# Reordering the first batch's adapter and the copies of its first weights

## The chip, the cores and the metric

The kernel runs on one NeuronCore of a Trainium2 chip. The metric is the device time of one execution in microseconds, as the median of a few executions. Five engines work side by side, each with its own instruction stream: TensorE (PE; PEld is its weight load), VectorE (DVE), ScalarE (ACT), GpSimd (POOL) and SyncE (SP). They order themselves with semaphores. DMAs are issued here by SyncE and ScalarE.

## What is computed

The input `x` is (4, 512, 256) in float32. Four stages, each with a residual, are applied one after the other; weights are picked by small index inputs, one index to a batch element:

```python
# L0: adapter of a language, then a layer norm
h = relu(x @ W1[lang] + b1[lang])                 # (512, 64)
a = x + h @ W2[lang] + b2[lang]                   # (512, 256)
x = x + layernorm(a) * gamma[lang] + beta[lang]
# L1: a linear layer of a subject
x = x + (x @ weight[subj].T + bias[subj])
# L2: two experts and three shared nets (256 -> 1024 -> 256, relu between), gated
x = x + sum_of_nets(x)
# L3: attention pooling with a prefix, postfix or cloze mask
x = x + masked_pooling(x)
```

Only the first batch element's L0 and L1, and the loading of its first L2 weights, are touched by the change.

## The kernel before

**Stages.** The four batch elements run one after the other. A batch is `SLOTS` = 40 slots of L2 work (5 nets times 8 chunks of 128 hidden units). In each slot TensorE computes one chunk of the hidden layer (`first_product`, into `ps_hid`) and, two slots later, what that chunk adds to the output (`second_product`, into `ps_net`). The L0 and L1 stages of the next batch and L3 of the one before are woven into the slots. All large products are made of three matmuls on split operands: each operand is a `hi` part (rounded to float32r) and a `lo` part (the rest), and hi·hi, lo·hi and hi·lo are summed. So every chunk of hidden values is split by ScalarE (`hid_hi`, with the relu) and VectorE (`hid_lo`), and every pair of weight chunks by ScalarE (`wi_hi`, `wo_hi`) and GpSimd (`wi_lo`, `wo_lo`).

**Weights.** SyncE loads them by halves of a net (four chunks, 512 KB of wi into `raw_wi` and 512 KB of wo into `raw_wo`), into two slots in turn (`load_half`, L458 to L471). A pair of chunks is split by `split_weights` on ScalarE (L1074) and GpSimd. The very first half is issued by ScalarE (L1175, L1176) in the prologue, and its two pairs are copied by `first_wi` and `first_wo`. SyncE waits for both transfers of that half (`raw_in[0]`, L484) before it issues the second half at L470; before that it has loaded the first batch's parameters (`load_params`, L422 to L430, which begins with two register loads of an index), the subject's index and bias (`load_subject`, L433 to L438, again two register loads) and the small resident arrays (`load_resident`).

**The prologue.** L0 and L1 of the first batch cannot be woven into anything, so each engine has a `prologue`. It works on two halves `h` of 256 rows, that is four row tiles `r` of 128 (half 0 has tiles 0 and 1, half 1 has 2 and 3):

- TensorE transposes x (`transpose_half`, L558), computes the adapter's first product of a half (`adapter_hidden`, L638, 64 output columns, float32 in four passes) and the second product of a tile (`adapted_rows`). Even tiles get x added by TensorE with an identity matmul (L646); odd tiles get it from VectorE. Before the change it does half 0's first product, tiles 0 and 1, then half 1's first product, tiles 2 and 3. Then it transposes the subject's weights (L565, L567), transposes the normalised rows of half 0, runs three warm-up matmuls on zeros (`keep_warm`, L687), and computes the subject product `x2_part` (L666) and the first chunks of L2 for each half.
- ScalarE copies the transposed x to SBUF (`x1T`, L1147), applies bias and relu (`adapter_hidden`, L1151, writes `hT`), adds beta to the transposed x (`x_beta`, L1155, writes `xbT`), normalises the even tiles (`normalise`, L1161), copies the transposed subject weights (L1183), splits the first weights (L1164, L1169) and evacuates the subject product as `x2T_hi` (L1194).
- VectorE computes the statistics of a tile (`statistics`, L1740 adds x for odd tiles, L1743), the variance of a half (`variance`, L1749 to L1753), normalises the odd tiles (L1758), adds the normalised values to `xbT` (`add_norm`, L1763, writes `x1T`) and writes `x2T_lo` (L1771).
- GpSimd computes `rstd` and `neg_shift` of a half (L1945, L1947), then `wi_lo` and `wo_lo` of the first weights.

**What sets the order.** It is written out by hand. Each engine's instructions run in program order; each step increments a semaphore, and `Steps` turns a step's name into the count to wait for, so the strings of names (`p_pe`, `p_act`, `p_dve`) must list the steps in the order in which each engine does them.

**The small parameters.** In the first slots of batch 0 VectorE computes gate probabilities and mask parameters (`parameters(slot)`, L1651 to L1705) on tiny tiles of 128x4. Each of these steps waits for the one before. The memset of `mix_done` (L1679) tells ScalarE that the experts' scales are ready, for which ScalarE waits before it writes `wo_hi` of an expert (L1085). VectorE does `hid_lo` of a slot (L1823) in between, in program order. GpSimd, after the third pair of weights, sets up constants (L1957 to L1971), and then goes on with the pairs.

## Time and profile before

| | us |
|---|---|
| median of 3 runs | 502.25 (502.12 to 503.63) |
| the profiled execution, its own time | 501.93 |
| its span, from the first to the last instruction | 500.1 |
| PE busy, share of the span | 493.7, 99% |
| DVE busy | 349.2, 70% |
| ACT busy | 260.9, 52% |
| POOL busy | 235.8, 47% |

The span is the stretch between the first and the last instruction; 1.83 us of the execution's time lie around it. Busy times overlap, since the engines run side by side. Matmuls are pipelined, so the busy time of a group of matmuls ends after the next group has begun; the spacing of starts tells the pace. Rows of a timeline give the start, the length, the engine, the line, the operation, output<-input with shapes, how many instructions were merged (x4), and in brackets how long the engine was idle before and who ended that. What ended a wait is inferred from semaphores.

### The profile page before, as it was taken

To read this page: it belongs to the slowest core of one execution; us is meant where nothing else is said; L and a number is where in the kernel's file an instruction comes from. 1 tells how busy PE (TensorE), PEld (TensorE's weight loads), DVE (VectorE), ACT (ScalarE), POOL (GpSimd) and SP (SyncE) were. 2 spreads that over 40 slices of the span, in tenths; PEclk is the share of its full clock that TensorE was granted. 3 is DMA by queue.
4 is the path that set the end of the run, shared out by engine and by line. 5 is a ranking of instruction groups with operands and counts; after the bars stand their busy time and mean duration, and the time that the engine had idled before them with its cause. 6 is when DMAs were issued, how large, how long until landed. Compare 5 with 4: busy or idle time off the path is not lost.

```text
span 500.1 us, 7007 instructions
## 1 busy us (share of the span) xinstructions
PE 493.7 (99%) x2327; PEld 408.6 (82%) x2327; DVE 349.2 (70%) x703; ACT 260.9 (52%) x507; POOL 235.8 (47%) x201
## 2 busy tenths in 40 slices
PE   8999999999999999999999999999999999999996
PEld 5788888888888888888888888888888888888984
DVE  5687226884687799785578689788468779644477
ACT  4655554443457574535346666444345757445234
POOL 1684455445354446444644437444535444745022
PEclk9999999999999999999999999999999999999999
DMA  5865454222265442422227453422222342330002
GB/s 156 185 184 148 111 154 142 86 85 85 86 128 141 116 112 86 127 83 89 80 90 185 105 178 107 127 84 85 85 85 85 102 109 84 102 132 22 0 1 84
DMA packets 77657, 52.97 MB, mean 106 GB/s; under 512 B 40758, under 2 KB 67382, under 8 KB 77622
## 3 DMA queue, kind: packets, MB, share of 16 engines
q1 hardware_dynamic: 75734, 50.44, 35.6%
q10 hardware_dynamic: 1888, 2.10, 1.4%
q8 instruction: 18, 0.29, 0.2%
q14 instruction: 17, 0.14, 0.1%
HBM read 48.33 MB, written 2.10 MB: 101 GB/s over the span
## 4 chain that ended last, share of the span: by engine, by line
PE 98%; DVE 1%; ACT 1%; issue 0%; POOL 0%; DVEq 0%
PE ps_hid L838 14%; PE ps_hid L839 14%; PE ps_hid L843 14%; PE ps_net L900 14%; PE ps_net L895 14%; PE ps_net L896 14%; PE ps_net L867 2%; PE ps_side L537 1%; PE ps_side L541 1%; PE ps_side L536 1%; PE ps_side L547 1%; PE ps_side L550 1%; PE ps_hid L687 1%; PE ps_side L730 1%; PE ps_net L666 1%; PE ps_hid L638 0%
## 5 line engine op out<-in xcount | busy, mean ns | idle before, releaser
L1915 POOL TENSOR_TENSOR wi_lo<-raw_wi,wi_hi 128x512 fp32r<-128x512 f32 x77 | 101.6, 1319 | 207.0 <-ACT wo_hi L1088 109.8
L1109 ACT ACTIVATE hid_hi<-ps_hid 128x512 fp32r<-128x512 f32 x160 | 95.5, 598 | 194.9 <-PE ps_hid L843 193.1
L1823 DVE SCALAR_TENSOR_TENSOR hid_lo<-ps_hid,hid_hi 128x512 fp32r<-128x512 f32 x160 | 109.8, 688 | 114.0 <-ACT hid_hi L1109 112.8
L838 PE MATMUL ps_hid<-x2T_hi,wi_lo 128*128 128x512 f32 (+1 forms) x332 | 125.8, 381 | 0.0
L839 PE MATMUL ps_hid<-x2T_hi,wi_hi 128*128 128x512 f32 (+1 forms) x332 | 125.3, 379 | 0.0
L895 PE MATMUL ps_net<-hid_hi,wo_hi 128*128 128x512 f32 x304 | 118.9, 391 | 0.0
L896 PE MATMUL ps_net<-hid_hi,wo_lo 128*128 128x512 f32 x304 | 118.4, 390 | 0.0
L1916 POOL TENSOR_TENSOR wo_lo<-raw_wo,wo_hi 128x512 fp32r<-128x512 f32 x77 | 104.1, 1352 | 0.0
L843 PE MATMUL ps_hid<-x2T_lo,wi_hi 128*128 128x512 f32 (+1 forms) x332 | 98.9, 379 | 0.0
L900 PE MATMUL ps_net<-hid_lo,wo_hi 128*128 128x512 f32 x304 | 94.0, 390 | 0.0
L839 PEld LDWEIGHTS ps_hid<-x2T_hi,wi_hi 128*128 128x128 f32 x332 | 62.5, 188 | 11.8
L838 PEld LDWEIGHTS ps_hid<-x2T_hi,wi_lo 128*128 128x128 f32 x332 | 62.5, 188 | 11.7
L843 PEld LDWEIGHTS ps_hid<-x2T_lo,wi_hi 128*128 128x128 f32 x332 | 61.3, 188 | 11.8
L900 PEld LDWEIGHTS ps_net<-hid_lo,wo_hi 128*128 128x128 f32 x304 | 57.0, 188 | 12.4 <-DVE hid_lo L1823 0.4
L895 PEld LDWEIGHTS ps_net<-hid_hi,wo_hi 128*128 128x128 f32 x304 | 57.1, 188 | 11.6
L896 PEld LDWEIGHTS ps_net<-hid_hi,wo_lo 128*128 128x128 f32 x304 | 57.1, 188 | 11.5
L1081 ACT ACTIVATE wi_hi<-raw_wi 128x512 fp32r<-128x512 f32 x78 | 48.8, 626 | 1.5 <-DMA raw_wo<-in_L_cond_expert_wo_dram 1.1
L1088 ACT ACTIVATE wo_hi<-raw_wo 128x512 fp32r<-128x512 f32 x46 | 28.6, 622 | 0.0
L1085 ACT ACTIVATE wo_hi<-raw_wo,par 128x512 fp32r<-128x512 f32 x32 | 23.0, 719 | 1.7 <-DVE mix_done L1679 1.7
L1086 ACT ACTIVATE raw_wo<-raw_wo,par 128x512 f32<-128x512 f32 x32 | 22.9, 716 | 0.0
L1383 DVE SCALAR_TENSOR_TENSOR x3T<-netT,gates,x3T 128x512 f32<-128x512 f32 x24 | 19.5, 854 | 0.1
L1811 DVE SCALAR_TENSOR_TENSOR gate_acc<-gate_w,netT,gate_acc 128x256 f32<-128x256 f32 x26 | 17.5, 673 | 1.8
(330 smaller groups left out, 502.7 us busy)
## 6 DMA issues: line engine op xcount, KB each, us to landing
raw_wi<-in_L_cond_share_wi_dram SPq DMA_DIRECT2D x23, 512.0 KB, 3.8
raw_wo<-in_L_cond_share_wo_dram SPq DMA_DIRECT2D x23, 512.0 KB, 4.8
raw_wi<-in_L_cond_expert_wi_dram SPq DMA_DIRECT2D x16, 512.0 KB, 3.8
raw_wo<-in_L_cond_expert_wo_dram SPq DMA_DIRECT2D x16, 512.0 KB, 4.8
next_x2T<-in_x_dram SPq DMA_DIRECT2D x24, 64.0 KB, 4.3
x_rows<-in_x_dram SPq DMA_DIRECT2D x3, 512.0 KB, 4.0
x_rows<-netT SPq DMA_DIRECT2D x48, 32.0 KB, 2.0
out_dram<-out_rows SPq DMA_DIRECT2D x5, 256.0 KB, 5.6
```

The lines of the kernel that those rows point to most:

```text
L838: mm(dst, wi_lo[:, w, k, c], x2T_hi[:, k, rows], start=(k == 0), stop=False)
L839: mm(dst, wi_hi[:, w, k, c], x2T_hi[:, k, rows], start=False, stop=False)
L843: last = mm(dst, wi_hi[:, w, k, c], x2T_lo[:, k, rows], start=False, stop=(k == KD - 1))
L895: mm(dst, wo_hi[:, w, q % 2, cols], hid_hi[:, slot], start=opens, stop=False)
L896: mm(dst, wo_lo[:, w, q % 2, cols], hid_hi[:, slot], start=False, stop=False)
L900: last = mm(dst, wo_hi[:, w, q % 2, cols], hid_lo[:, slot], start=False, stop=closes)
L1081: fn(wi_hi[:, w], raw_wi[:, half % 2, :, c], ACT.Copy)
L1088: fn(wo_hi[:, w], raw, ACT.Copy).then_inc(w_hi_ready, 1)
L1109: fn(hid_hi[:, ring(b, q)], ps_hid[:, ring(b, q)], ACT.Relu).then_inc(hid_hi_ready, 1)
L1823: v.scalar_tensor_tensor(out=hid_lo[:, ring(b, q)], in0=ps_hid[:, ring(b, q)], scalar=0.0, in1=f32(hid_hi[:, ring(b, q)]), op0=ALU.max, op ...
L1915: g.tensor_tensor(wi_lo[:, w], raw_wi[:, half % 2, :, c], f32(wi_hi[:, w]), ALU.subtract)
L1916: g.tensor_tensor(wo_lo[:, w], raw_wo[:, half % 2, t], f32(wo_hi[:, w]), ALU.subtract).then_inc(w_lo_ready, 1)
```

## The change

On TensorE the first product of half 1 follows directly on that of half 0; then come the second products in the order tile 1, 0, 3, 2. The wait for hT of a half moves from the even tile to the odd one, which is now first. VectorE takes the statistics in the order 1, 0, variance of half 0, 3, 2, normalise of half 0, variance of half 1. ScalarE does both halves' relu first and `x_beta` of both after, issues the loads of the subject's weights and of the first wi before it waits for the first product, and issues the load of the first wo after the relu of half 0. The first wi and wo get a semaphore each (`first_raw_wi`, `first_raw_wo`), so that the counts of `raw_in[0]` start with the third half. The first copy of wi moves ahead of the normalising of half 1. The three warm-up matmuls become two.

```diff
-    WARM_XT, WARM_SUBJ = 6, 3
+    WARM_XT, WARM_NORM = 6, 2
...
+        first_raw_wi, first_raw_wo = sem("first_raw_wi"), sem("first_raw_wo")
...
-        p_pe = Steps(sem("p_pe"), "xT0 xT1 hid0 adapt0 adapt1 hid1 adapt2 adapt3 subj_wT normT0 normT1 y0 y1")
-        p_act = Steps(sem("p_act"), "xT0 xT1 hid0 xb0 hid1 xb1 norm0 subj_wT norm1")
-        p_dve = Steps(sem("p_dve"), "stats0 sum1 stats1 aggr0 var_eps0 stats2 norm0 sum3 stats3 aggr1 var_eps1 x1T00 x1T01 norm1 x1T10 x1T11")
+        p_pe = Steps(sem("p_pe"), "xT0 xT1 hid0 hid1 adapt1 adapt0 adapt3 adapt2 subj_wT normT0 normT1 y0 y1")
+        p_act = Steps(sem("p_act"), "xT0 xT1 hid0 hid1 xb0 xb1 norm0 subj_wT norm1")
+        p_dve = Steps(sem("p_dve"), "sum1 stats1 stats0 aggr0 var_eps0 sum3 stats3 stats2 norm0 aggr1 var_eps1 x1T00 x1T01 norm1 x1T10 x1T11")
...
                         load_resident()
-                        sp.wait_ge(raw_in[0], 32)
+                        sp.wait_ge(first_raw_wi, 16)
+                        sp.wait_ge(first_raw_wo, 16)
...
                 for h in range(2):
                     adapter_hidden(h)
-                    for r in (2 * h, 2 * h + 1):
+                for h in range(2):
+                    for r in (2 * h + 1, 2 * h):
                         adapted_rows(r)
...
                 normalised_rows(0)
-                keep_warm(WARM_SUBJ, warm)
+                keep_warm(WARM_NORM, warm)
...
                 if r % 2 == 0:
-                    if r == 2:
-                        pe.wait_ge(p_act.sem, p_act.at(0, "hid0"))
                     mm(adapted_bank(r), ident[:], x_rows[:, r], start=True, stop=False)
+                else:
                     pe.wait_ge(p_act.sem, p_act.at(0, f"hid{r // 2}"))
-                    if r == 0:
-                        pe.wait_ge(zeros_ready, 3)
-                        pe.wait_ge(w2_in, 16)
-                        pe.wait_ge(b2_in, 16)
+                if r == 1:
+                    pe.wait_ge(zeros_ready, 3)
+                    pe.wait_ge(w2_in, 16)
+                    pe.wait_ge(b2_in, 16)
...
-                act.wait_ge(raw_in[half % 2], 32 * ((HALVES // 2) * b + half // 2 + 1))
+                if not (isinstance(b, int) and b == 0 and half == 0):
+                    act.wait_ge(raw_in[half % 2], 32 * ((HALVES // 2) * b + half // 2 + half % 2))
...
+            act.dma_start(subj_w[:], ...).then_inc(subj_in, 16)
+            net, cols = NET_AT[0] - 2, slice(0, F // 2)
+            act.dma_start(raw_wi[:, 0], ...).then_inc(first_raw_wi, 16)
             act.wait_ge(b1_in, 16)
             adapter_hidden(0)
-            act.dma_start(subj_w[:], ...).then_inc(subj_in, 16)
-            net, cols = NET_AT[0] - 2, slice(0, F // 2)
-            act.dma_start(raw_wi[:, 0], ...).then_inc(raw_in[0], 16)
-            act.dma_start(raw_wo[:, 0], ...).then_inc(raw_in[0], 16)
+            act.dma_start(raw_wo[:, 0], ...).then_inc(first_raw_wo, 16)
+            adapter_hidden(1)
             act.wait_ge(beta_in, 16)
             x_beta(0)
-            adapter_hidden(1)
             x_beta(1)
             normalise(0)
             act.wait_ge(p_pe.sem, p_pe.at(0, "subj_wT"))
             fn(first_subj_wT.rearrange("p k d -> p (k d)"), ps_net[:, 2], ACT.Copy).then_inc(p_act.sem, 1)
+            act.wait_ge(first_raw_wi, 16)
+            first_wi(0)
             normalise(1)
-            act.wait_ge(raw_in[0], 32)
-            first_wi(0)
+            act.wait_ge(first_raw_wo, 16)
             first_wo(0)
             first_wi(1)
             first_wo(1)
...
                 def variance(h):
...
-                    here(f"stats{2 * h + 1}")
+                    here(f"stats{2 * h}")
...
+                statistics(1)
                 statistics(0)
-                statistics(1)
                 variance(0)
+                statistics(3)
                 statistics(2)
                 normalise(0)
-                statistics(3)
                 variance(1)
```

## Rows read from the trace of the kernel before

**Rows 1.** The page's first part: busy us, share of the span, instructions.

```profile
PE 493.7 (99%) x2327; PEld 408.6 (82%) x2327; DVE 349.2 (70%) x703; ACT 260.9 (52%) x507; POOL 235.8 (47%) x201
```

**Rows 2.** Timeline, 5 to 20 us: start, us, engine, line, operation, [idle before <- releaser].

```profile
5.60 1.08 PE L638 MATMUL ps_hid<-x1T,w 128*64 128x256 f32 x4 [0.18 <-ACT x1T L1147]
7.30 1.13 PE L652 MATMUL ps_net<-w2b,hT 65*128 65x256 f32 x4
8.11 0.43 DVE L1743 BATCH_NORM_STATS2 stats<-ps_net 128x6 f32<-128x256 f32 x1 [3.12 <-PE ps_net L652]
8.36 1.08 PE L638 MATMUL ps_hid<-x1T,w 128*64 128x256 f32 x4
9.75 0.16 DVE L1753 TENSOR_SCALAR var_eps<-aggr 128x2 f32<-128x2 f32 x1
11.07 0.56 ACT L1161 ACTIVATE norm<-ps_net,neg_shift,rstd 128x256 f32<-128x256 f32 x1 [0.41 <-POOL neg_shift L1947]
12.74 0.87 DVE L1763 SCALAR_TENSOR_TENSOR x1T<-ps_side,gamma,xbT 128x256 f32<-128x256 f32 x2
13.36 1.10 PE L666 MATMUL ps_net<-x1T,out_rows 128*128 128x256 f32 x4 [0.26 <-DVE x1T L1763]
13.64 0.41 DVE L1758 TENSOR_SCALAR norm<-norm,aggr,rstd 128x256 f32<-128x256 f32 x1
13.91 0.56 ACT L1161 ACTIVATE norm<-ps_hid,neg_shift,rstd 128x256 f32<-128x256 f32 x1 [1.26 <-POOL neg_shift L1947]
14.62 0.63 PE L558 MATMUL ps_side<-ident,norm 128*128 128x128 f32 x4 [0.16 <-ACT norm L1161]
16.46 0.82 ACT L1194 ACTIVATE x2T_hi<-ps_net,subj_b 128x256 fp32r<-128x256 f32 x2
17.88 0.84 ACT L1194 ACTIVATE x2T_hi<-ps_net,subj_b 128x256 fp32r<-128x256 f32 x2 [0.60 <-PE ps_net L666]
```

**Rows 3.** Timeline, 21 to 39 us, of ScalarE, POOL and VectorE.

```profile
21.96 0.63 ACT L1081 ACTIVATE wi_hi<-raw_wi 128x512 fp32r<-128x512 f32 x1 [0.35 <-DMA raw_wo<-in_L_cond_share_wo_dram]
...
29.95 1.29 POOL L1916 TENSOR_TENSOR wo_lo<-raw_wo,wo_hi 128x512 fp32r<-128x512 f32 x1
...
31.89 0.72 ACT L1085 ACTIVATE wo_hi<-raw_wo,par 128x512 fp32r<-128x512 f32 x1 [1.65 <-DVE mix_done L1679]
...
37.26 1.28 POOL L1916 TENSOR_TENSOR wo_lo<-raw_wo,wo_hi 128x512 fp32r<-128x512 f32 x1
...
37.36 1.21 DVE L1692 SCALAR_TENSOR_TENSOR par<-onehot,jcol,par 128x4 f32<-128x4 f32 x1
...
38.80 0.69 DVE L1823 SCALAR_TENSOR_TENSOR hid_lo<-ps_hid,hid_hi 128x512 fp32r<-128x512 f32 x1
```

**Rows 4.** The chain that ended last, 36 to 40 us: start, us, what.

```profile
36.87 0.45 PE ps_net L900 x2
...
39.59 0.69 PE ps_net L900 x2
```

**Rows 5.** Waits of SyncE's queue, 0 to 24 us: total us, times, longest us.

```profile
SPq L470 <- DMA raw_wo<-in_L_cond_share_wo_dram: 0.4, 1, 0.4
```

**Rows 6.** Timeline of the DMA issues of the first two halves of wi.

```profile
7.35 0.50 ACTq L1175 DMA_DIRECT2D raw_wi<-in_L_cond_share_wi_dram  x1
...
13.84 0.37 SPq L470 DMA_DIRECT2D raw_wi<-in_L_cond_share_wi_dram  x1
```

**Rows 7.** The page's DMA issues: KB each, median us from issue to landing.

```profile
raw_wi<-in_L_cond_share_wi_dram ACTq DMA_DIRECT2D x1, 512.0 KB, 5.0
```

**Rows 8.** Line L433, all batches: ns min/median/max, first and last start.

```profile
L433 SPq TENSOR_LOAD <-in_itok_B_dram_ptr x4: 1244/2490/2636, 6.6 to 296.4; - x4
L433 SPq TENSOR_LOAD <-in_itok_B_dram x4: 458/462/818, 7.9 to 299.2; - x4
```

**Rows 9.** Timeline of the two bursts of warm-up matmuls.

```profile
1.32 2.74 PE L687 MATMUL ps_hid<-edge_diag 128*128 128x512 bf16 x6 [1.32 <-DVE edge_diag L1847]
...
12.29 0.81 PE L687 MATMUL ps_hid<-edge_diag 128*128 128x512 bf16 x3
```

More of the change, by code:

```diff
@@ L1169, in first_wo @@
                 fn(wo_hi[:, p], raw_wo[:, 0, 2 * p:2 * (p + 1)], ACT.Copy).then_inc(w_hi_ready, 1)
+            act.dma_start(subj_w[:], L1_weight[bass.ds(subj, 1)].rearrange("o (k p) d -> p (o k) d", p=P)).then_inc(subj_in, 16)
+            net, cols = NET_AT[0] - 2, slice(0, F // 2)
+            act.dma_start(raw_wi[:, 0], L2_share_wi[net:net + 1, :, cols].rearrange("o (k p) f -> p (o k) f", p=P)).then_inc(first_raw_wi, 16)
             act.wait_ge(b1_in, 16)
             adapter_hidden(0)
-            act.dma_start(subj_w[:], L1_weight[bass.ds(subj, 1)].rearrange("o (k p) d -> p (o k) d", p=P)).then_inc(subj_in, 16)
-            net, cols = NET_AT[0] - 2, slice(0, F // 2)
-            act.dma_start(raw_wi[:, 0], L2_share_wi[net:net + 1, :, cols].rearrange("o (k p) f -> p (o k) f", p=P)).then_inc(raw_in[0], 16)
-            act.dma_start(raw_wo[:, 0], L2_share_wo[net:net + 1, cols].rearrange("o (c p) d -> p (o c) d", p=P)).then_inc(raw_in[0], 16)
+            act.dma_start(raw_wo[:, 0], L2_share_wo[net:net + 1, cols].rearrange("o (c p) d -> p (o c) d", p=P)).then_inc(first_raw_wo, 16)
+            adapter_hidden(1)
             act.wait_ge(beta_in, 16)
             x_beta(0)
-            adapter_hidden(1)
             x_beta(1)
```

## The prediction

> **What bounds the kernel now.** I read four views, in this order. The page's first part says which engine is full: TensorE is busy for 493.7 us of a span of 500.1 [rows 1], so a gain can only come from what TensorE idles or waits, and the change touches only the first 20 us. The timeline of those 20 us comes next: the reader is to see which start stands right behind a wait. TensorE begins the adapter's first product of half 0 at 5.60 and that of half 1 at 8.36. The normalising of half 1 is late: ScalarE sat idle for 1.26 us before it at 13.91, and TensorE's transposes of half 1 start behind it at 14.62 [rows 2]. So half 1 is the late one, by what its statistics cost after 8.36. Then the chain of waits further on: TensorE's product with hid_lo at 39.59 takes 0.69 us where the one before it took 0.45 [rows 4], a stall of 0.24 us outside the changed code. And last the queue that loads weights, SyncE's: it waited 0.4 us for the first half of wo before it could issue the second half of the weights at 13.84 [rows 5, 6].
>
> **The sum for the prologue, half 0.** The first product of half 1 (four passes) now stands between hid0 and the adapter rows. The wait for hT of half 0, which ended at 7.30, was partly idle for TensorE; the four passes of half 1, 0.22 us apart and with the array already set to 64 columns, come at 6.5 to 7.2, and the adapter can begin at 7.47. The first adapter tile (now the odd one) took from 7.30 to 8.11 to reach VectorE and now reaches it at about 8.28 [rows 2]. The same VectorE operations stand between that and var_eps of half 0: 8.11 to 9.91 is 1.80 us, so it ends at 10.08, 0.17 later, and ScalarE's normalising goes from 11.07 to 11.24. The identity pass of tile 0 hid the wait for hT before; it now lies behind tile 1 and is covered by VectorE's 0.8 us of work on tile 1. ScalarE ends at 11.80, and with the 0.15 us between that and TensorE's start (13.91 plus 0.56 to 14.62) the transposes run from 11.96 to about 12.60. Before, VectorE could take x1T of half 0 only at 12.74, held by its own statistics of half 1; now those are done and it starts at 12.70. TensorE's first subject product moves from 13.36 to 13.32: a gain of 0.04 us.
>
> **Half 1.** VectorE goes on with tiles 3 and 2 without a wait, because their products are ready by 9.5 and 10.4. By the 1.80 us of half 0, begun at 9.99 and with one normalising of about 0.3 (its pace in the pipeline) in between, var_eps of half 1 is done at 12.0 to 12.1. From there to ScalarE's start POOL takes 1.16 us or less (9.91 to 11.07), so ScalarE starts at 13.1 to 13.2 instead of 13.91 and is done at 13.7 [rows 2]. VectorE's share of it is queued behind x1T of half 0: 12.70 plus 0.80 plus 0.41 is 13.91 [rows 2]. Both are ready before TensorE has issued the four passes it began at 13.32, so the transposes of half 1 follow at 14.26 instead of 14.62, and what is behind them moves by 0.39 with the refill of the array that the wait cost. **The prologue's sum is 0.39 us.**
>
> **The weight copies.** ScalarE reaches the first copy of wi at about 12.2. Issued with subj_w right after the second x1T copy, wi leaves at about 6.0 instead of 7.35, and lands 5.0 us later, at 11.0 [rows 6, 7]. The copies end at 15.1 instead of 16.46, so the first evacuation of x2T no longer waits for ScalarE: 15.84 [rows 2]. TensorE's short wait behind that in the first halves goes, but then the last part of half 1 decides: its evacuation began at 17.88, as soon as TensorE was done, and it keeps its length. It moves by 0.39 and no more, so I cost the copies' move at nothing beyond the 0.39. If ScalarE were still behind, it would hold 0.6 us. Three semaphore waits are split or moved, one warm-up pass is dropped (0.22 us, in a gap), and no instruction of the steady part changes: nothing.
>
> **Where the 0.39 us goes.** This is what decides, so I followed the stall at 39.59 back. It is TensorE waiting for VectorE's hid_lo of 38.80. VectorE came to that only after the parameter operation of 37.36, which takes 1.21 us on 128x4 elements and ends within 0.03 us of POOL's operation of 37.26 (1.28 us) [rows 3]. POOL's work comes behind ScalarE's weight copies, those behind wo_hi at 31.89, which waited for VectorE's mix_done, and that behind parameter steps that stood beside POOL's operation of 29.95; POOL's series and VectorE's both begin with ScalarE's copy of 21.96, which waited for a DMA: the second half of wo [rows 3]. From that landing to 39.5 there is no step that waits for TensorE. So TensorE meets hid_lo at 39.5 however early it arrives: it comes 0.39 earlier and stalls 0.24 plus 0.39. The weight pairs before it (POOL's series for slot 6 ends at 31.24) hang on the same landing. **What moves the end is when the second half of wo lands.** The most that could be gained is 0.63 us.
>
> **The landing.** SyncE issues that load at 13.84 because it waited 0.4 us [rows 5, 6]; the first wo is now issued about 1 us sooner and should be in by 13, so this wait goes: 0.37 earlier. Against it: SyncE's two loads of the subject index (L433), from 6.59 to 8.68 before, now run beside the transfers of subj_w and wi. In this run the pair took 1.24 and 0.82 us in the prologue, and 2.64 and 0.46 at the most in later batches, where weights were in flight [rows 8]. Bounds: 0 (or a gain of 0.3, were each load as short as its shortest row allows) and 1.04 us later, the sum of both longest against now. I take 0.3, nearer the prologue's rows since only ScalarE's queue is full there. The sum is 0.37 minus 0.3, so 0.07 us earlier, with ends at 0.63 earlier and 0.67 later.
>
> The trace shows the operations of 37.26 and 37.36 ending together [rows 3]. The Trainium skill, SBUF — State Buffer, Who interferes with whom, says that VectorE and GpSimd share a pair of ports as an exclusive lock, and that the one that comes second blocks fully. By that rule, with which the trace agrees, the order of the two starts decides: a step of VectorE that came first would take its own 0.2 us instead of 1.2, and hid_lo would come up to 1 us sooner, which is one way into rival A. A rule that speaks against the change is in DMA: Bandwidth & Descriptors, Issuing engines are not separate DMA queues: transfers issued from different engines run on the same DMA engines and interleave. By it, wi sent sooner from ScalarE slows what SyncE has under way; no row here shows the two together, and the sum would be rival B's.
>
> **The numbers.** The profiled execution took 501.93 us, its span 500.1, so 1.83 lie around it; it stands 0.32 under the median of 502.25. 501.93 minus 0.07 is 501.86, and on the scale of the median 502.2 us.
>
> **Rivals.** A: the chain from the landing is earlier after all (SyncE not slowed, or a step of VectorE of about 0.2 us, as the small one of 9.75 [rows 2] takes, starts ahead of POOL's operation and not behind it), and the gain survives. For it: SyncE's wait of 0.4 is real [rows 5]. Against: everything in the chain is in program order. Gain 0.3 to 0.63: 501.6 to 501.9. B, on the other side: the second half of the weights lands later. Its place is L433 and its price up to 1.04 us against the 0.37; it decides from where SyncE arrives at L470 after 13.84, that is once the two index loads take over 0.4 us more than now. It then shows in full, as a longer stall at hid_lo: up to 0.67, 502.9. C: TensorE's clock falls in the prologue. The burst of six at 1.32 takes 0.46 us each, the three at 12.29 take 0.27 [rows 9]: the lower and the upper of the two levels (1.2 and 2.4 GHz). The lower one was over by the four passes of 5.60, which take the 1.08 us of those of 8.36 [rows 2], so it held for at most 4.3 us. The change makes an idle stretch of 0.7 us before 11.96 and one of 0.4 before 13.32. Another such spell at half pace costs at most 2.1 us and I take 1.8, of which 0.24 to 0.6 would vanish in the stall: 503.5 to 503.8. Against: TensorE is busy in most of every such stretch. D: the change does not do what it says, because wi lands after 12.8 and its copy delays normalising; then the prologue gains less than 0.39, and the end is the same as in the forecast, since the stall swallows either.
>
> **How the numbers follow.** Forecast, with D: 0.63, its own range 501.9 to 502.5. A 0.18, B 0.14, C 0.04, anything else 0.01. The range 501.6 to 502.9 holds the first three by their bounds; one of the three runs shown lies 1.4 us above the others, so I widen it to 501.5 and 503.2. A bound of 0.3% is 1.5 us, about what a measurement can tell: faster than that needs more than the 0.63 that there is, 0.02; slower is C (its upper end, or C together with B), 0.04; the rest is same, 0.94.
>
> **What would show it.** Right: adapter products of half 1 near 6.5 and statistics without a gap; TensorE's transposes of half 1 near 14.3; the first full product at 20.4 instead of 20.81; then a wait of about 0.8 instead of 0.4 for hid_lo near 39.5, within 0.1 us of where it was plus the shift of SyncE's L470. Wrong: a hid_lo that comes 0.3 or more earlier without L470 being earlier; a stall of TensorE elsewhere; transposes of half 1 still behind ScalarE, which would be a wi landing late.

## The result and the profile after

The changed kernel takes 503.43 us (median, 502.96 to 503.76), the kernel before, run beside it, 502.45 (502.09 to 503.63): a ratio of 1.0016 with a 95% interval of 1.0009 to 1.0024, that is 0.5 to 1.2 us slower. The forecast was 502.2, with a range to 503.2. The profiled execution of the changed kernel took 503.46 us with a span of 501.6, 1.5 more than the span before.

The page of the changed kernel, first the busy times (to be held against [rows 1]), then two groups of TensorE's instructions, with what idled before them at the end:

```profile
PE 494.0 (98%) x2326; PEld 409.0 (82%) x2326; DVE 349.2 (70%) x703; ACT 260.6 (52%) x507; POOL 235.8 (47%) x201
...
L840 PE MATMUL ps_hid<-x2T_hi,wi_lo 128*128 128x512 f32 (+1 forms) x332 | 125.9, 381 | 0.5 <-POOL wo_lo L1920 0.5
...
L902 PE MATMUL ps_net<-hid_lo,wo_hi 128*128 128x512 f32 x304 | 94.0, 390 | 0.3 <-DVE hid_lo L1827 0.3
```

TensorE waits in two places, and both lie behind the prologue: for GpSimd's `wo_lo`, and for a `hid_lo`. (Lines of the changed kernel are one to four higher than before.) The prologue, from the timeline of 4 to 22 us, answers [rows 2]:

```profile
5.70 1.49 PE L641 MATMUL ps_hid<-x1T,w 128*64 128x256 f32 x4
...
8.80 0.42 DVE L1744 TENSOR_TENSOR norm<-ps_net,x_rows 128x256 f32<-128x256 f32 x1 [3.80 <-PE ps_net L654]
...
11.74 0.56 ACT L1164 ACTIVATE norm<-ps_net,neg_shift,rstd 128x256 f32<-128x256 f32 x1 [1.74 <-POOL neg_shift L1951]
...
12.45 0.63 PE L560 MATMUL ps_side<-ident,norm 128*128 128x128 f32 x4 [0.71 <-DVE var_eps L1757]
...
13.43 1.27 POOL L1953 TENSOR_TENSOR wi_lo<-raw_wi,wi_hi 128x512 fp32r<-128x512 f32 x1
13.52 0.56 ACT L1164 ACTIVATE norm<-ps_hid,neg_shift,rstd 128x256 f32<-128x256 f32 x1 [0.20 <-POOL neg_shift L1951]
13.82 1.10 PE L668 MATMUL ps_net<-x1T,out_rows 128*128 128x256 f32 x4 [0.31 <-DVE x1T L1767]
13.98 0.87 DVE L1762 TENSOR_SCALAR norm<-norm,aggr,rstd 128x256 f32<-128x256 f32 x1
14.95 0.63 PE L560 MATMUL ps_side<-ident,norm 128*128 128x128 f32 x4
18.21 0.84 ACT L1198 ACTIVATE x2T_hi<-ps_net,subj_b 128x256 fp32r<-128x256 f32 x2 [0.83 <-PE ps_net L668]
21.13 0.39 PE L840 MATMUL ps_hid<-x2T_hi,wi_lo 128*128 128x512 f32 x1
```

Three things are to be seen. The first four passes take 1.49 us instead of 1.08: TensorE was still slow when they began, in code that no edit had touched. Half 1 follows sooner on half 0 (transposes at 12.45 and 14.95, 2.50 apart; before, 11.85 and 14.62, 2.77). And VectorE's normalising at 13.98 takes 0.87 us instead of 0.41, beside GpSimd's `wi_lo` of 13.43, which used to come later. Together they make the first full product 0.32 us later (21.13 against 20.81).

The later stretch, from the timeline of 21 to 42 us, answers [rows 3, 4]:

```profile
23.45 0.63 ACT L1084 ACTIVATE wi_hi<-raw_wi 128x512 fp32r<-128x512 f32 x1 [1.52 <-DMA raw_wo<-in_L_cond_share_wo_dram]
...
27.28 0.50 PE L840 MATMUL ps_hid<-x2T_hi,wi_lo 128*128 128x512 f32 x1 [0.52 <-POOL wo_lo L1920]
...
33.37 0.72 ACT L1088 ACTIVATE wo_hi<-raw_wo,par 128x512 fp32r<-128x512 f32 x1 [1.90 <-DVE mix_done L1683]
...
38.75 1.28 POOL L1920 TENSOR_TENSOR wo_lo<-raw_wo,wo_hi 128x512 fp32r<-128x512 f32 x1
...
38.85 1.22 DVE L1696 SCALAR_TENSOR_TENSOR par<-onehot,jcol,par 128x4 f32<-128x4 f32 x1
...
40.31 0.69 DVE L1827 SCALAR_TENSOR_TENSOR hid_lo<-ps_hid,hid_hi 128x512 fp32r<-128x512 f32 x1
...
41.05 0.73 PE L902 MATMUL ps_net<-hid_lo,wo_hi 128*128 128x512 f32 x2 [0.27 <-DVE hid_lo L1827]
```

All steps of the chain that [rows 3] showed come 1.5 us later, without a change among them: 21.96, 31.89, 37.36 and 38.80 became 23.45, 33.37, 38.85 and 40.31. So the chain was moved as a whole, at its start. And its start is SyncE. First its two index loads (the line's own view: ns min/median/max, first start), then, from the timeline, ScalarE's issue of the first wi and SyncE's of the second, as in [rows 6, 8]:

```profile
L434 SPq TENSOR_LOAD <-in_itok_B_dram_ptr x1: 1810/1810/1810, 6.6 to 6.6; - x1
L434 SPq TENSOR_LOAD <-in_itok_B_dram x1: 1708/1708/1708, 8.4 to 8.4; - x1
```

```profile
6.37 0.49 ACTq L1176 DMA_DIRECT2D raw_wi<-in_L_cond_share_wi_dram  x1
...
15.03 0.40 SPq L471 DMA_DIRECT2D raw_wi<-in_L_cond_share_wi_dram  x1
```

The pair took 3.52 us instead of 2.06, and SyncE came to the second wi at 15.03 instead of 13.84. Its wait of 0.4 us for the first half [rows 5] is gone, as forecast, and it is 1.19 later all the same.

The span closes from these rows. The first full product is 0.32 later. TensorE's wait at 27.28 costs 0.52, and 0.27 for a first pass of 0.50 where the steady ones follow each other by 0.23. The one at 41.05 costs 0.27, and 0.28 for a pair of 0.73 instead of 0.45. Less the 0.24 of before [rows 4], that is 1.4 of the 1.5; the rest lies in delays of less than 0.1 us each in the slots behind these two waits.

### The profile page after: what moved, and what is told of

The parts are those of the page before. It is cut to its first block, busy times and chain, and to the rows that moved or that the text cites. A ratio compares the mean times of both kernels' runs of the same rounds, so it can differ in the third digit from the quotient of the medians.

```text
span 501.6 us, 7006 instructions
## 1 busy us (share of the span) xinstructions
PE 494.0 (98%) x2326; PEld 409.0 (82%) x2326; DVE 349.2 (70%) x703; ACT 260.6 (52%) x507; POOL 235.8 (47%) x201
## 4 chain that ended last, share of the span: by engine, by line
PE 91%; DVE 3%; SPq 3%; DMA 2%; issue 1%; ACT 1%; DVEq 0%; ACTq 0%
PE ps_hid L840 14%; PE ps_hid L841 14%; PE ps_hid L845 14%; PE ps_net L902 13%; PE ps_net L897 13%; PE ps_net L898 13%; PE ps_net L869 2%; DMA raw_wo<-in_L_cond_share_wo_dram 2%; SPq L434 1%; DVE hid_lo L1827 1%; PE ps_side L539 1%; DVE pick L1680 1%; PE ps_side L543 1%; PE ps_side L538 1%; PE ps_side L549 1%
## 5 line engine op out<-in xcount | busy, mean ns | idle before, releaser
L902 PEld LDWEIGHTS ps_net<-hid_lo,wo_hi 128*128 128x128 f32 x304 | 57.0, 188 | 12.7 <-DVE hid_lo L1827 0.7
```

The source lines that it names most:

```text
L902: last = mm(dst, wo_hi[:, w, q % 2, cols], hid_lo[:, slot], start=False, stop=closes)
```

## The experiments

Three theories were set against each other. Index theory: the first wi, sent sooner, slows SyncE's index loads, so the second half of the weights is issued and lands later, and the chain to hid_lo of slot 6 with it. Port theory: the slow normalising beside `wi_lo` is what costs. Order theory: the new order of the adapter is what costs. All numbers first, in one table. The columns: the two index loads together; SyncE's issue of the second wi; ScalarE's first copy of that half; hid_lo of slot 6; TensorE's first full product; the span; the median and the ratio to the kernel before, run beside it (at 502.36 to 502.47), with its interval.

| kernel | index loads | second wi | copy | hid_lo | full product | span | median | ratio |
|---|---|---|---|---|---|---|---|---|
| before | 2.06 | 13.84 | 21.96 | 38.80 | 20.81 | 500.1 | 502.45 | 1 |
| changed | 3.52 | 15.03 | 23.45 | 40.31 | 21.13 | 501.6 | 503.43 | 1.0016 (1.0009 to 1.0024) |
| e1_issues_back | 1.84 | 13.38 | 21.75 | 38.63 | 20.46 | 499.9 | 502.33 | 1.0001 (0.9991 to 1.0011) |
| e2_issues_alone | 3.01 | 14.47 | 23.04 | 39.89 | 20.99 | 501.2 | 503.01 | 1.0010 (1.0000 to 1.0020) |
| e3_bias_by_scalar | none | 13.72 | 22.04 | 38.89 | 20.90 | 500.2 | 502.36 | 0.9995 (0.9985 to 1.0005) |
| e4_order_alone | 2.00 | 13.55 | 22.33 | 39.19 | 20.40 | 500.5 | 502.79 | 1.0011 (0.9998 to 1.0024) |
| e5_back_spread | 1.99 | 13.53 | 22.32 | 34.83 | 20.64 | 500.0 | 501.89 | 0.9989 (0.9978 to 1.0000) |
| e6_spread_alone | 1.51 | 14.02 | 22.73 | 35.19 | 21.27 | 500.3 | 502.09 | 0.9990 (0.9982 to 0.9999) |
| e7_bias_no_wait | none | 11.44 | 21.90 | 38.74 | 21.20 | 500.2 | 501.45 | 0.9979 (0.9970 to 0.9987) |
| e8_two_more_loads | 2.00 + 2.46 | 16.38 | 25.13 | 41.93 | 20.74 | 503.2 | 505.79 | 1.0066 (1.0053 to 1.0079) |
| e9_no_wait_spread | none | 10.71 | 22.21 | 34.68 | 21.51 | 500.6 | 501.69 | 0.9982 (0.9973 to 0.9991) |
| e10_copy_after_norm | none | 10.57 | 21.15 | 33.62 | 20.45 | 499.4 | 501.41 | 0.9975 (0.9967 to 0.9984) |
| e11_before_no_wait | none | 11.69 | 23.02 | 39.87 | 22.33 | 501.4 | 503.14 | 1.0007 (0.9998 to 1.0015) |
| e12_only_wi_later | 2.05 | 13.71 | 22.49 | 39.38 | 20.96 | 500.5 | 502.35 | 0.9999 (0.9991 to 1.0008) |

**Which part costs: e1 and e2.** In the first, the changed kernel's three issues go back behind the relu of half 0; in the second, only they move, in the kernel before.

```diff
-            act.dma_start(subj_w[:], ...).then_inc(subj_in, 16)
-            act.dma_start(raw_wi[:, 0], ...).then_inc(first_raw_wi, 16)
             act.wait_ge(b1_in, 16)
             adapter_hidden(0)
+            act.dma_start(subj_w[:], ...).then_inc(subj_in, 16)
+            act.dma_start(raw_wi[:, 0], ...).then_inc(first_raw_wi, 16)
             act.dma_start(raw_wo[:, 0], ...).then_inc(first_raw_wo, 16)
```

> The changed kernel, with only ScalarE's three DMA issues (subject's weights, first wi, first wo) put back to where the kernel before has them, behind the relu of half 0. Index theory (the earlier transfers slow SyncE's two index loads, so the second half of the weights is issued 1.2 us later and the chain that hangs on its landing comes 1.5 later): the two loads take 1.3 and 0.8 us again instead of 1.8 and 1.7, SyncE issues the second wi at 13.5 to 13.9 instead of 15.03, hid_lo of slot 6 begins within 0.3 us of 38.8, and the time is that of the kernel before within 0.3 us, 502.2 to 502.7. Rival, the port theory (VectorE's normalising of half 1 takes 0.87 instead of 0.41 us beside GpSimd's first wi_lo) and rival, the order theory (the new order of the adapter's products is what costs): both parts are still in this kernel, so it stays near 503.4.

> The kernel before, with only ScalarE's DMA issues moved sooner as in the change (subject's weights and first wi before the wait for the first product, first wo behind the relu of half 0). Order of the adapter and of the weight copies as before. Index theory: the two index loads take 3.2 to 3.6 us together, the second wi is issued at 14.8 to 15.2, hid_lo of slot 6 begins near 40.3, and the time is 503.2 to 503.6. Port and order theories: neither of their parts is in this kernel, so it is at the kernel before's 502.45 within 0.3 or faster.

With the issues back, the loads take 1.84 us, hid_lo is at 38.63, and the time is 502.33, the kernel before's. With the issues alone it is 503.01: 0.5 of the 1.0 us, with neither the new order nor the early copy in it. That is less than the index theory expected: the loads took 3.01 us and not 3.2 to 3.6, hid_lo came at 39.89 and not near 40.3, and the time is below 503.2. The loads of e2_issues_alone:

```profile
L433 SPq TENSOR_LOAD <-in_itok_B_dram_ptr x1: 2310/2310/2310, 6.6 to 6.6; - x1
L433 SPq TENSOR_LOAD <-in_itok_B_dram x1: 699/699/699, 8.9 to 8.9; - x1
```

Here the first of the two is the long one (2.31), in the changed kernel both are. The interval of e2 touches 1.000, so its median alone would not settle it; the rows and e1 do. The port and order theories fall as the cause of the loss, since e1 has both their parts and not the loss.

The traffic of all DMA engines goes with the loads. From 6.6 to 7.6 us, beside the first load, it was 214 GB/s in e2_issues_alone and 2 to 32 in before, e1, e6, e12 and the changed kernel. From 8.6 to 9.6, beside the second load of the changed kernel, it was 374 there. Traffic alone does not say how long a load takes, though: the second load of e2 ran beside some 356 GB/s and took 0.70.

**Which transfer slows them: e12.** The subject's weights (256 KB) stay early, at 5.95, the first wi (512 KB) goes back to 7.11.

```diff
             act.dma_start(subj_w[:], ...).then_inc(subj_in, 16)
-            act.dma_start(raw_wi[:, 0], ...).then_inc(first_raw_wi, 16)
             act.wait_ge(b1_in, 16)
             adapter_hidden(0)
+            act.dma_start(raw_wi[:, 0], ...).then_inc(first_raw_wi, 16)
             act.dma_start(raw_wo[:, 0], ...).then_inc(first_raw_wo, 16)
```

> The changed kernel, with the subject's weights still issued sooner (before the relu of half 0), but the first wi behind it as in the kernel before. It tells which transfer slows SyncE's index loads. If it is wi (512 KB, issued at 6.4): the pair takes 1.9 to 2.3 us as in the kernel before, the second wi is issued at 13.4 to 13.9 and the time is 502.2 to 502.7. If it is the subject's weights (256 KB, issued at 5.95, just before the loads begin at 6.6): the pair takes 3.0 to 3.5, the second wi is issued at 14.5 to 15.0 and the time is 503.0 to 503.5.

```profile
L434 SPq TENSOR_LOAD <-in_itok_B_dram_ptr x1: 1390/1390/1390, 6.6 to 6.6; - x1
L434 SPq TENSOR_LOAD <-in_itok_B_dram x1: 656/656/656, 8.1 to 8.1; - x1
```

2.05 us together, 502.35, as expected: with wi issued 0.7 us later the loads are as short as before, though the subject's weights stay early. So wi is needed for the slowdown. Whether it does it alone is open, for no kernel has wi early and the subject's weights late.

**Does the end follow SyncE: e8.** The kernel before, with one more pair of index loads behind the first.

```diff
                 subj = sp.value_load(subj_row[0:1, bass.ds(i, 1)], ...)
+                if isinstance(i, int) and i == 0:
+                    sp.value_load(subj_row[0:1, bass.ds(1, 1)], ...)
```

> The kernel before, with one more pair of register loads of an index on SyncE behind the first pair (its value is not used). It changes nothing but the time at which SyncE goes on. Index theory: the pair takes 1.5 to 2.6 us with its check, the second wi is issued at 15.3 to 16.3 instead of 13.84 (the wait of 0.37 takes part of it), hid_lo of slot 6 moves by the same 1.5 to 2.5, and the span with it, 501.6 to 502.6. Rival, the time of the landing is not what sets the end: within 0.3 of the kernel before's 500.1.

The second wi went out 2.54 later, hid_lo came 3.13 later, and the span grew by 3.1. The size was more than the 1.5 to 2.5 expected: the extra pair and its check put off the bias issue by 2.9 us, and the half came another 0.6 late. The median of its five runs is 3.4 over the kernel before. The mechanism is the expected one. TensorE's two waits, from its timeline of 22 to 46 us:

```profile
28.90 0.50 PE L840 MATMUL ps_hid<-x2T_hi,wi_lo 128*128 128x512 f32 x1 [2.54 <-POOL wo_lo L1918]
...
42.68 0.73 PE L902 MATMUL ps_net<-hid_lo,wo_hi 128*128 128x512 f32 x2 [0.28 <-DVE hid_lo L1825]
```

In the table, span less hid_lo is 461.3 in before, changed, e1 to e4 and e8, and 461.1 in e12: wherever TensorE waits for that hid_lo, its start fixes the end, whatever the prologue did.

**Is the prologue's gain real, and where did it go: e4, e5, e6.** e4 is the kernel before with only the new order. e5 is e1 with VectorE's parameter steps taken from in front of hid_lo, e6 the kernel before with the same edit:

```diff
-                if slot in (5, 6):
+                if slot in (9, 10, 11, 12):
...
-                    for r in (2 * (slot - 5), 2 * (slot - 5) + 1):
+                    for r in (slot - 9,):
```

> The kernel before with only the new order of the adapter's work (both first products in a row, tile 1 before 0 and 3 before 2, VectorE and ScalarE in the matching order): DMA issues, the place of the first weight copy and three warm-up matmuls as before. Index theory and my forecast for this part: the first full product of L2 starts 0.2 to 0.4 us sooner than in the kernel before where the clock rises at the same time, the second wi is issued as before (13.5 to 13.9), and the end does not move: within 0.3 of the kernel before. Order theory: near 503.4. Port theory: like the kernel before, since the first wi_lo comes behind the normalising.

> The kernel of e1_issues_back, with VectorE's parameter steps of slots 5 and 6 (twelve tiny operations, of which six take 1.2 us beside GpSimd) spread over slots 9 to 12, three to a slot, so that no hid_lo stands behind them near 38 us. Swallow theory (the prologue gained 0.35 us, and TensorE's stall at hid_lo of slot 6 ate it): the stall of 0.41 us in e1_issues_back goes, nothing takes its place, and the gain appears: span 499.4 to 499.6, and 0.3 to 0.4 us under e6_spread_alone. Rival, the prologue gained nothing: the same as e6_spread_alone within 0.1.  Rival, another stall takes its place (a hid_lo of slots 9 to 12): span as in e1_issues_back, 499.9 or more.

> The kernel before, with only those parameter steps spread over slots 9 to 12. The stall of 0.24 us at hid_lo of slot 6 goes: span 499.8 to 499.9, median 0.2 to 0.6 under the kernel before, and the runs scatter less, since the end no longer follows the landing of the second half of the weights while that lands by 22 us. Rival, the stall moves to a later slot: no gain.

In e4 the first full product is at 20.40, 0.41 sooner than before, and the first adapter pass at 5.60, as before; the forecast had said 0.39. The end did not gain in this execution, because the half was copied late (22.33) and hid_lo held TensorE. Its median, 502.79, lies 0.3 over the kernel before, at the edge of what was expected, and its interval (0.9998 to 1.0024) shows neither a loss nor its absence; that the order is not what costs is e1's to show. With the steps out of the way hid_lo of slot 6 comes at 34.83 and 35.19, some four microseconds sooner, the stall behind it is gone in both e5 and e6, and both are 0.3 to 0.5 us under the kernel before; e6's runs lie within 501.86 to 502.71, those of the kernel before, beside them, within 501.97 to 503.98. Between e5 and e6 the medians differ by 0.2, which their scatter does not bear out. Their spans missed the expected 499.4 to 499.6 and 499.8 to 499.9, each for a reason that a row shows: in e6 TensorE's clock rose late (first full product at 21.27; 500.1 plus 0.46 less 0.24 is 500.3), in e5 the half landed at 22.3 and TensorE lost 0.3 us at the first two pairs of it. So in e5 another stall did take the place of the one at hid_lo, as its rival had it, but not at the hid_lo of slots 9 to 12. The gain of the prologue is seen at the first full product; at the end it is not shown.

**The copy's place: e4 against e5, then e10.** e5 has the first copy of wi ahead of the normalising of half 1, e4 behind it; the adapter's passes start at the same times in both. From the timelines of 11 to 22 us, e4_order_alone:

```profile
11.95 0.63 PE L560 MATMUL ps_side<-ident,norm 128*128 128x128 f32 x4 [0.56 <-DVE var_eps L1757]
...
13.47 0.41 DVE L1762 TENSOR_SCALAR norm<-norm,aggr,rstd 128x256 f32<-128x256 f32 x1
14.17 1.28 POOL L1953 TENSOR_TENSOR wi_lo<-raw_wi,wi_hi 128x512 fp32r<-128x512 f32 x1 [1.19 <-ACT wi_hi L1167]
...
20.40 0.40 PE L840 MATMUL ps_hid<-x2T_hi,wi_lo 128*128 128x512 f32 x1
```

and e5_back_spread:

```profile
11.94 0.63 PE L560 MATMUL ps_side<-ident,norm 128*128 128x128 f32 x4 [0.55 <-DVE var_eps L1757]
...
12.93 1.27 POOL L1953 TENSOR_TENSOR wi_lo<-raw_wi,wi_hi 128x512 fp32r<-128x512 f32 x1
...
13.47 0.88 DVE L1762 TENSOR_SCALAR norm<-norm,aggr,rstd 128x256 f32<-128x256 f32 x1
...
20.64 0.40 PE L840 MATMUL ps_hid<-x2T_hi,wi_lo 128*128 128x512 f32 x1
```

The same operation at the same time takes 0.41 with GpSimd idle and 0.88 with `wi_lo` running, and the first full product starts 0.24 later. The stretch from the transposes of half 0 to that product does not depend on when the clock rose, and sorts the kernels: 8.96 us in before, e2, e6 and e8 (old order), 8.68 to 8.70 in the changed kernel and the six others with the new order and the early copy, 8.45 in e4 and 8.48 in e10 (new order, late copy). So the early copy costs 0.24. The new order is worth 0.4: 0.51 by this stretch, less 0.10 by which its transposes start later. The Trainium skill, SBUF — State Buffer, Who interferes with whom, has the two engines lock each other out of a pair of ports, so that the one that comes second waits. The rows agree: VectorE ends at 14.35, just behind GpSimd's recorded end of 14.20. Whether it was blocked all that time they cannot tell.

**A way out: e3, e7, e11.** ScalarE holds the subject's index already, so it can load the bias, and SyncE's two loads fall away (e3). e7 also drops SyncE's wait for the first half. e11 is the kernel before with both edits of e7.

```diff
+            with nc.allow_non_contiguous_dma(reason="one element to a partition"):
+                act.dma_start(subj_b[:], L1_bias[bass.ds(subj, 1)]...).then_inc(subj_b_in, 16)
...
             load_params(0)
-            load_subject(0)
```

```diff
                         load_resident()
-                        sp.wait_ge(first_raw_wi, 16)
-                        sp.wait_ge(first_raw_wo, 16)
```

> The changed kernel, but the first subject's bias is loaded by ScalarE, which has the index in a register already, behind its relu of half 1; SyncE's two index loads of the first batch and its issue of the bias fall away. Index theory: SyncE reaches its wait for the first wo before that lands, issues the second wi at 12.0 to 12.4, 3 us sooner than in the changed kernel; hid_lo of slot 6 begins at 37.3 to 38.2, TensorE's stalls at 27, 33 and 41 us go, and the time is 501.5 to 502.1, under both kernels. Port and order theories: both their parts are in, so it is no better than 503.1.

> The kernel of e3_bias_by_scalar (bias loaded by ScalarE), without SyncE's wait for the first wi and wo, which took 2.9 us there: it sends the second half as soon as the small arrays are issued, at 10.7 to 11.1 instead of 13.72. Index theory in its full form (what sets the end is the landing of the second half): ScalarE's first copy of it starts 1.5 to 3 us sooner than at 22.04, if the first wo (landed near 13.7) comes less than 1 us later for the traffic; hid_lo of slot 6 comes at 37 to 38, no stall is left, span 499.5 to 499.8. Rival, traffic theory (the transfers share what the DMA engines move, so the first wo or the bias is delayed by as much as the second half gains): the first weight copies or x2T_hi come 1 us or more later, the first full product too, and the span is 500.5 or more.

> The kernel before (its order of the adapter, of the weight copies and of ScalarE's other issues), with only the two edits of e7_bias_no_wait: the bias loaded by ScalarE, behind its three other issues, and SyncE's wait for the first half of the weights gone. Index theory: no stall hangs on the landing any more, so this is under the kernel before too, 501.6 to 502.0, and e7_bias_no_wait (501.45) is below it by what its prologue is worth once nothing swallows it, 0.39 less 0.24 for the port: 0.1 to 0.3. Rival, the landing was worth nothing to the kernel before: 502.3 or more.

e3 took the loss away (502.36) and no more. Its second wi went out at 13.72, not at 12.0 to 12.4, for SyncE now sent its small arrays beside the first weights, these landed later (wo 6.6 us after its issue, 4.7 in the changed kernel), and it waited for them, as its waits of 0 to 24 us show:

```profile
SPq L486 <- DMA raw_wo<-in_L_cond_share_wo_dram: 2.9, 1, 2.9
```

Without that wait (e7) the second wi leaves at 11.44, ScalarE's copy of 21.90 waits for no DMA, no stall is left, and the median is 501.45, 1.0 under the kernel before and 2.0 under the changed one. That falls within neither of my expected stories: the span is 500.2, since the clock rose late in this execution, and the first wo was not late. Nor was the early issue worth 2.3 us at the other end: the second wo landed at 21.78, against 22.02 in e3, for it now took 9.8 us and not 7.9. The same edits in the kernel before went wrong, and my expectation with them. There the first half is issued later, and the second came on top of it. ScalarE's timeline in e11_before_no_wait:

```profile
15.90 0.63 ACT L1162 ACTIVATE wi_hi<-raw_wi 128x512 fp32r<-128x512 f32 x1 [1.19 <-DMA raw_wo<-in_L_cond_share_wo_dram]
...
18.00 1.55 ACT L1194 ACTIVATE x2T_hi<-ps_net,subj_b 128x256 fp32r<-128x256 f32 x4
```

The first copies wait 1.19 us, x2T_hi stands behind them at 18.00 (first part 16.46 before [rows 2]), and the kernel takes 503.14, 0.8 over the kernel before by the medians (its interval, 0.9998 to 1.0015, just holds 1). The first wo took 8.0 us there, 5.9 in the kernel before and 6.6 in e7. So SyncE's wait protected the first half in the old kernel and was needless in the new one. That the early issue makes the difference is argued: the order of the adapter and of the copies differs as well. What e3 and e7 do show is that the early issue without the index loads is no loss.

**The best version: e9 and e10.** e9 is e7 with the steps spread as in e5, e10 is e9 with the first copy behind the normalising.

```diff
-            act.wait_ge(first_raw_wi, 16)
-            first_wi(0)
             normalise(1)
+            act.wait_ge(first_raw_wi, 16)
+            first_wi(0)
             act.wait_ge(first_raw_wo, 16)
```

> The kernel of e7_bias_no_wait with the parameter steps of slots 5 and 6 spread over slots 9 to 12 as in e5_back_spread. With the second half early, and no hid_lo behind those steps, nothing before slot 10 waits for the landing. In runs in which TensorE's clock rises late, e7_bias_no_wait has no stall to lose and this is equal to it; in those in which it rises early this is up to 0.4 us faster. Expected: 501.0 to 501.5, under e7_bias_no_wait's 501.45 by 0 to 0.3. Rival, the spread steps themselves hold up a later hid_lo: 501.6 or more.

> The kernel of e9_no_wait_spread, with the first copy of wi put back behind ScalarE's normalising of half 1 (the wait for the first wo stays behind it). Port theory, in the size that e4 against e5 gives (first full product at 20.40 against 20.64 with the clock rising alike): VectorE's normalising of half 1 takes 0.41 instead of 0.88 us, since GpSimd's first wi_lo then comes behind it; the first full product starts 0.2 to 0.25 us sooner than in e9_no_wait_spread at an equal clock, and the time is 0.1 to 0.3 lower. Rival: the copies come later by as much and x2T_hi waits for ScalarE, no gain.

e9 is at 501.69, not under e7, and in the range of the rival that the spread steps hold up a later hid_lo. Its trace speaks against that: TensorE's slots follow each other by 2.72 us from the second full product on, as in e7, and its first full product is the latest of the new order (21.51), with the clock. With no stall at hid_lo left to remove, nothing is shown of a gain. e10 is at 501.41, 0.28 under e9, as expected, though that is within the scatter of the two; its stretch from the transposes (11.97) to the first full product is 8.48, against 8.69 in e9:

```profile
20.45 0.40 PE L837 MATMUL ps_hid<-x2T_hi,wi_lo 128*128 128x512 f32 x1
```

It is 0.8 to 1.7 us faster than the kernel before by its interval.

## Why the prediction was wrong

**The prologue's sum of 0.39: right for the order, wrong for the copies.** e4 gives 0.41 for the new order alone, and its steps are those of the sum: ScalarE's first normalising at 11.24, the transposes at 11.95 and 14.25, the full product at 20.40, where 11.24, 11.96, 14.26 and 20.4 were forecast. "The copies' move at nothing" was the wrong step: I had asked only whether ScalarE would be late for x2T_hi and had not followed who else uses the copied tile. GpSimd's `wi_lo` starts as soon as it is there, and VectorE's normalising then takes 0.87 instead of 0.41. The price is 0.24, and 0.17 of the gain is left. It changed nothing at the end.

**The stall that swallows: right.** That the end hangs on hid_lo near 39.5, this on the landing of the second half, and nothing between on TensorE, is what the constant 461.3 shows, over 3 us of shift. The wait of 0.4 at SyncE went, as forecast. This holds only as long as TensorE waits for that hid_lo; in e7 it no longer did.

**The landing: this is the term that failed.** The sum was 0.37 earlier less S, with S = 0.3 taken and 1.04 as its bound. S was 1.46 in the changed kernel's profile, and the issue came 1.19 later instead of 0.07 earlier. It was rival B as described, with its place and its point of decision (0.4 us), and I gave it 0.14. Three choices were wrong. I took the value near the prologue's own rows, "since only ScalarE's queue is full there", although that queue was just what the change brought forward. The bound was called "the sum of both longest" and was not: 1.04 is the longest pointer load with the longest value load of the later batches (2.64 plus 0.46, less 2.06). With the 0.82 of the prologue the same rows [rows 8] give 1.40. And I looked at one line only. Loads of the same kind by another line, L481, stand in the trace of before, 4 us behind SyncE's issue of the second wi:

```profile
L481 SPq TENSOR_LOAD <-in_itok_B_dram_ptr x1: 1416/1416/1416, 18.0 to 18.0; - x1
L481 SPq TENSOR_LOAD <-in_itok_B_dram x1: 1654/1654/1654, 19.4 to 19.4; - x1
```

Here the value load takes 1.65 us, as the 1.71 of the changed kernel. The longest of each, 2.64 and 1.65, would have put the bound at 2.2 us, above the 1.46 that came. By the Trainium skill, DMA: Bandwidth & Descriptors, Issuing engines are not separate DMA queues, transfers issued by two engines run on the same DMA engines. The forecast had quoted it and left it to the rival. e12 against the changed kernel now shows the price of wi for the loads (2.05 us with wi at 7.11, 3.52 with wi at 6.37). The page speaks of DMAs; that register loads meet them on the same path no run here shows.

**A second stall that I did not list.** At most 0.67 was to be lost, all at hid_lo. In the changed kernel TensorE waits at 27.28 as well, for the pair of weights that comes first from the late half, and loses 0.79 there, more than the 0.55 at 41.05. A stall of TensorE elsewhere was one of the signs of being wrong that the forecast had named. I had noted that the pairs hang on the same landing and had not asked by how much they were ahead. In before, GpSimd is done with that pair at 25.73 (24.44 plus 1.29) and TensorE comes to it at 26.28: 0.55 us. With 1.5 us of shift that was gone.

**How much of the 1.5 is real.** The medians differ by 0.98, the two profiles by 1.5. From issue of the second wi to ScalarE's first copy of that half the ten kernels in which that copy waited for a DMA took 8.12 to 8.79 us, and the 8.12 is that of before's profile. So the profile of before was probably on the lucky side, by some 0.5 us: its execution took 501.93, the median is 502.45. I had put it at 0.32. The clock adds to it: a late rise costs the kernel before its full length beyond 0.24 us of stall, while the changed kernel's longer waits absorb it. That would fit its narrower runs (0.8 us between first and last, against 1.5), but it is argued, not shown.

**The other rivals.** A needed an earlier chain; it did not come in the changed kernel. In e5, e6, e9 and e10, with the steps out of its way, hid_lo of slot 6 came 3.6 to 5.2 us earlier than in before, and the medians of all four, and of e7, are under the kernel before. C (the clock falls a second time) did not occur: after the rise, all passes of the adapter run at the upper level. D did not occur either, for wi landed by 10.6 and was copied at 12.7.

## What to carry to other kernels

Before a transfer is sent sooner, look at what the other queues do in those microseconds, small register loads above all, and follow who waits behind them. Take the price of such a load from every line that has one, not from the line in question alone. Here 1.0 us gained for the issue of a 512 KB transfer cost 1.5 us on another engine's queue. A stall that several parts of a change could move should be traced to its source first; only the edit that moves the source counts. And a wait that holds traffic back may be protecting something: the same two edits gave 2.0 us in the changed kernel and none in the kernel before, where the median rose by 0.8.

## What the runs showed of the hardware

The index loads vary widely. In the prologue the same pair took 1.51 to 2.06 us in seven kernels, and 3.01 and 3.52 in the two with wi issued at 5.8 and 6.4. In the later batches the first of the two took 2.4 to 2.6 us as a rule and the second 0.46 [rows 8]; at 18 us in before, behind the issue of the second half, they took 1.42 and 1.65.

TensorE's rise from the lower to the upper of its two levels (1.2 and 2.4 GHz) falls at different moments in the fourteen profiles, although the kernels have the same TensorE code up to there. In the two profiles of before and after, the adapter's first four passes took 1.08 and 1.49 us. The eight transposes ahead of them, in the changed kernel's timeline of 4 to 7 us:

```profile
3.85 1.92 PE L560 MATMUL ps_side<-ident,x_rows 128*128 128x128 f32 x8
```

In before they took 1.57: there they start 0.21 us apart at first and 0.11 apart at the end, while in the changed kernel all start 0.21 apart. TensorE had been busy from the warm-up burst on in both, but for the 0.18 us of [rows 2]. The column of the granted clock shows 1.00 in every one of these microseconds, in both kernels, so the level is to be read from the length of the passes and not from that column. Between e1 and e9, which have the same order and the same place of the copy, this moved the first full product by 1.05 us (20.46 and 21.51), more than twice what the new order gave.
